# First phase of a conv, attention and FFN kernel: mask and scores in 64x64 array tiles, state matmuls behind them

## What is computed

```
t = circulant_inverse @ x                      # channel mixing, tokens x 128
h = layernorm(t)
Q, K = elu(h Wq) + 1, elu(h Wk) + 1            # 8 heads of 16
V = h Wv
out = causal linear attention:
      num_t = Q_t . sum_{s<=t} K_s V_s,  den_t = Q_t . sum_{s<=t} K_s
t = t + (num / den) Wo
t = t + FFN(layernorm(t))                      # weights merged per batch by a gate, 128 -> 512 -> 128, layernorm
```

## Time and profile before

| | us |
|---|---|
| median of 3 runs | 775.72 |
| lowest and highest | 775.37, 778.26 |
| span of the profiled execution | 776.8 |
| PE busy | 724.4 (93%) |
| DVE busy | 675.7 (87%) |
| ACT busy | 655.0 (84%) |
| POOL busy | 537.7 (69%) |

### The profile page before, as it was taken

One profiled execution on the slowest core, in us unless ns is written; L12 is line 12 of the kernel. 1 busy time (PEld: TensorE's weight loads), 2 busy tenths in 40 slices (PEclk: granted clock), 3 DMA queues, 4 the chain that ended last, 5 costly groups with the idle time before them and its releaser, 6 DMA issues. The chain is left out here.

```text
span 776.8 us, 38919 instructions
## 1 busy us (share of the span) xinstructions
PE 724.4 (93%) x11938; PEld 541.6 (70%) x11938; DVE 675.7 (87%) x2614; ACT 655.0 (84%) x1860; POOL 537.7 (69%) x1167
## 2 busy tenths in 40 slices
PE   4899989999999999999999999868999999999994
PEld 2566667777677777677777776657777788777773
DVE  5798979999999999999999999856889978898983
ACT  4688989999999999999999999745788886888883
POOL 3798979999999999999999999620333330333332
PEclk9999999999999999999999999988999999999997
DMA  4657765565665565565566564410122220222221
GB/s 142 112 117 120 125 119 132 135 138 126 135 142 128 131 141 131 128 138 134 126 138 134 125 146 105 97 33 27 40 76 79 80 81 16 83 81 81 81 81 68
DMA packets 202341, 82.57 MB, mean 106 GB/s; under 512 B 176076, under 2 KB 189551, under 8 KB 202232
## 3 DMA queue, kind: packets, MB, share of 16 engines
q1 hardware_dynamic: 202296, 81.99, 45.8%
HBM read 22.69 MB, written 17.30 MB: 51 GB/s over the span
## 5 line engine op out<-in xcount | busy, mean ns | idle before, releaser
L864 DVE SCALAR_TENSOR_TENSOR scores_lo<-p_a,scores_hi 128x512 f16<-128x512 f32 x256 | 176.1, 688 | 4.6 <-ACT scores_hi L750 1.1
L750 ACT ACTIVATE scores_hi<-p_a 128x512 f16<-128x512 f32 x256 | 156.4, 613 | 19.1 <-PE p_a L591 12.8
L1403 POOL TENSOR_TENSOR ffn_rstd_shift<-ffn_rstd_shift,consts 128x4 f32<-128x4 f32 x32 | 36.8, 1150 | 111.4 <-DVE ffn_rstd_shift L1361 111.4
L968 POOL CAST qk_parts<-qk_f 128x256 f16<-128x256 f32 x256 | 108.9, 427 | 6.0 <-issue 4.0
L978 POOL TENSOR_TENSOR qk_parts<-qk_f,qk_parts 128x128 f16<-128x128 f32 x256 | 104.0, 427 | 0.9
L1185 PE MATMUL psb<-merged_W_of_batch,h_hi 128*128 128x128 f16 x512 | 95.3, 222 | 2.2 <-DVE h_lo L1339 1.5
L1339 DVE TENSOR_TENSOR h_lo<-h_f,h_hi 128x512 f16<-128x512 f32 x128 | 95.9, 789 | 0.6 <-ACT h_hi L1241 0.6
L1187 PE MATMUL psb<-merged_W_of_batch,h_lo 128*128 128x128 f16 x512 | 94.9, 221 | 0.0
L1186 PE MATMUL psb<-merged_W_of_batch,h_hi 128*128 128x128 f16 x512 | 94.9, 221 | 0.0
L1230 ACT ACTIVATE h_f<-psb,merged_b_of_batch 128x512 f32<-128x512 f32 x128 | 87.1, 712 | 7.7 <-PE psb L1166 6.0
L608 PE MATMUL p_o<-v_parts,scores_hi 128*128 128x17 f16 x1024 | 90.1, 171 | 2.0 <-issue 0.2
(11 more groups left out here) (214 smaller groups left out, 2846.9 us busy)
## 6 DMA issues: line engine op xcount, KB each, us to landing
x_f<-in_x SPq DMA_DIRECT2D x32, 256.0 KB, 3.1
t_rows<-t SPq DMA_DIRECT2D x64, 128.0 KB, 2.1
t_back<-t_rows SPq DMA_DIRECT2D x32, 256.0 KB, 2.6
out<-out_tile SPq DMA_DIRECT2D x32, 256.0 KB, 2.0
tv_share<-in_L_ffn_tv_W SPq DMA_DIRECT2D x32, 128.0 KB
qkT_parts<-qk_parts SPq DMA_TRANSPOSE x128, 3.1
zT_hi_lo<-z_parts SPq DMA_TRANSPOSE x128, 2.3
merged_W<-in_L_ffn_W SPq DMA_DIRECT2D x2, 256.0 KB, 4.3
```

The costliest lines, as they stand in the source:

```text
L750: nc.scalar.activation(ah[:, t % 2, cols], p_a[:, cols], ACT.Relu).then_inc(ahi_ready[eo], 1)
L864: nc.vector.scalar_tensor_tensor(al[:, t % 2, cols], p_a[:, cols], 0.0, ah[:, t % 2, cols], ALU.max, ALU.subtract).then_inc(alo_ready[eo], 1)
L968: nc.gpsimd.tensor_copy(dst, src.unsqueeze(2).broadcast_to([P, NH, 2, DH])).then_inc(done, 1)
```

## The change

In the scores stage mask and scores are made in 64x64 tiles of the array. Keys are split in halves c = 0 (keys 0 to 63 of the tile) and c = 1 (keys 64 to 127). The mask is written only to the two diagonal blocks, four matmuls of 64x256 in place of two of 128x512. The scores are sixteen matmuls in place of eight: keys 0 to 63 against all 128 queries, keys 64 to 127 against queries 64 to 127. The block of late keys against early queries is never written; DVE clears partitions 64 to 127 of p_a once at the start of the phase (semaphore scores_cleared), and its zeros stay. In TENSOR_ORDER the scores stage now stands ahead of state. The waits for all four parts of the tile before (hi and lo of both halves) stand ahead of the first mask matmul. ACT, DVE and GpSimd lists, and the size of what they read, are the same.

```diff
@@ -39,7 +39,7 @@
 
 
 
-TENSOR_ORDER = [("state", 3), ("scores", 4), ("turn_out", 6), ("conv", 0), ("values", 5), ("out_project", 6),
+TENSOR_ORDER = [("scores", 4), ("state", 3), ("turn_out", 6), ("conv", 0), ("values", 5), ("out_project", 6),
                 ("project", 0), ("gate", 13)]
 SCALAR_ORDER = [("normalise", 10), ("relu_qk", 2), ("split_x", 0), ("tv_hi", 0), ("read_t1", 7), ("gate_relu", 14),
                 ("state_hi", 3), ("exp_qk", 1), ("scores_hi_0", 4), ("copy_out", 6), ("scores_hi_1", 4), ("v_hi", 1)]
...
@@ -578,21 +578,31 @@
 
                     def scores(b, t):
                         n = TILES * b + t
+                        read = n if isinstance(n, int) else pe.to_reg(n)
+                        turned = 32 * b + 16 * (t // 4 + 1)
+                        turned = turned if isinstance(turned, int) else pe.to_reg(turned)
+                        pe.wait_ge(scores_cleared, 1)
                         for eo in range(2):
-                            at_least(pe, ahi_ready[eo], n)
-                            at_least(pe, alo_ready[eo], n)
-                            mm(p_a[:, eo * 512:(eo + 1) * 512], identb[:, :],
-                               maskb[:, :].unsqueeze(1).broadcast_to([P, NP, P]),
-                               start=True, stop=False, skip_group_check=True)
-                        pe.wait_ge(qk_turned[t % 4], 32 * b + 16 * (t // 4 + 1))
+                            at_least(pe, ahi_ready[eo], read)
+                            at_least(pe, alo_ready[eo], read)
+                        for c in range(2):
+                            for eo in range(2):
+                                r, k = slice(64 * eo, 64 * eo + 64), slice(64 * c, 64 * c + 64)
+                                o = p_a[k, eo * 512:(eo + 1) * 512].rearrange("p (a q) -> p a q", a=NP)[:, :, k]
+                                mm(o, identb[r, r], maskb[r, r].unsqueeze(1).broadcast_to([64, NP, 64]),
+                                   start=True, stop=False, skip_group_check=True)
+                        pe.wait_ge(scores_cleared, 1)
+                        pe.wait_ge(qk_turned[t % 4], turned)
                         for a in range(NP):
-                            for eo in range(2):
-                                r, c0 = 64 * eo, eo * 512 + a * P
-                                last = mm(p_a[:, c0:c0 + P],
-                                          qkT[r:r + 64, t % 4, 1, a, :], qkT[r:r + 64, t % 4, 0, a, :],
-                                          start=False, stop=True, skip_group_check=True)
-                                if a == NP - 1:
-                                    last.then_inc(sc_done[eo], 1)
+                            for c in range(2):
+                                for eo in range(2):
+                                    r, k = slice(64 * eo, 64 * eo + 64), slice(64 * c, 64 * c + 64)
+                                    c0 = eo * 512 + a * P
+                                    last = mm(p_a[k, c0 + 64 * c:c0 + P],
+                                              qkT[r, t % 4, 1, a, k], qkT[r, t % 4, 0, a, 64 * c:P],
+                                              start=False, stop=True, skip_group_check=True)
+                                    if a == NP - 1 and c:
+                                        last.then_inc(sc_done[eo], 1)
 
                     def values(b, t):
                         n = TILES * b + t
@@ -896,6 +906,7 @@
                         dve.wait_ge(bn2, upto)
                         nc.vector.bn_aggr(st2[:, t % 4, 6:8], st2[:, t % 4, 0:6]).then_inc(mv2, 1)
 
+                    nc.vector.memset(p_a[64:P, :], 0.0).then_inc(scores_cleared, 1)
                     nc.vector.memset(p_s[:, :], 0.0).then_inc(state_cleared, 1)
                     def merged_w1(slot):
                         if slot == 0:
```

More of the change, by code:

```diff
@@ L390, in build @@
             (conv_done, in_done, bn1, mv1, ve1, rstd1, vhi_ready, exp_ready, relu_ready, vlo_ready,
-             qk_ready, qhi_ready, khi_ready, lo_ready, su_done, state_cleared, sh_ready, sp_ready,
+             qk_ready, qhi_ready, khi_ready, lo_ready, su_done, state_cleared, scores_cleared, sh_ready, sp_ready,
              av_done, den1, den2, o_ready, ot_done, oT_ready, wo_done,
@@ L395, in build @@
                     "conv_done in_done bn1 mv1 ve1 rstd1 vhi_ready exp_ready relu_ready vlo_ready "
-                    "qk_ready qhi_ready khi_ready lo_ready su_done state_cleared sh_ready sp_ready "
+                    "qk_ready qhi_ready khi_ready lo_ready su_done state_cleared scores_cleared sh_ready sp_ready "
                     "av_done den1 den2 o_ready ot_done oT_ready wo_done "
```

## The result

The changed kernel takes 825.77 us (median of 4 runs, 824.03 to 830.74), the kernel before 776.99 in the same comparison; the ratio is 1.0635, 95% interval 1.0601 to 1.0670. Slower, by 49 us; 824 was forecast. The profiled execution has a span of 828.9 us; it is the slowest of the four, 5 us above their median.

A forecast was written before the change was run, and what follows sets the result against it. Bound: p_a's round trip, lengthened by state matmuls, state_hi and exp_qk. Steady 90 x 4.04 + 13 x 4.33 = 419.9 against 379.4, +40.5; +5 earlier slots, +3 ends: +48.5 on 776.8, 825.3; median 1.1 lower, 824 us; range 784 to 852.

The forecast's parts named there:

- the round trip of p_a: Single-buffered score tile passing PE, ACT, DVE, back to the next mask: 3.18 us before, 4.04 with the new order.
- The walk: First-phase loop timed from mask start T through scores, state, state_hi, exp_qk and scores parts back to PE: 4.04 us.
- the clock: Rival: TensorE idling lowers its granted clock, adding up to 0.3 us a loop, up to 851 us; 0.11 shared with serial tiles.
- the term for steps of the sequencer and handing over: On TensorE, score matmuls handed over by T + 0.40, then four steps of 0.38 us: state matmuls at T + 0.78.
- The slots ahead: The 20 uneven slots before the steady ones: 20 x (4.04 - 3.80) = +5 us.
- the last few: The last few slots with scores, counted together with the first two: +3 us.
- One sign of being wrong: On TensorE: the forecast is wrong if state matmuls start within 0.5 us of the mask.
- The rival of prepared steps (786 us): TensorE's sequencer prepares steps behind the blocked mask: state matmuls at T + 0.87 end, loop 3.71 us, 786 us; chance 0.15.
- Tiles in turn (870 us): TensorE's 64x64 tiles run one after another: loop 4.49 us, about 870 us; chance 0.11 shared with slow clock.
- The gain that gets through (764 us): state_hi does not hold back scores_hi_0 on ACT; TensorE's saving shows until GpSimd's 3.57 us binds: 764 us; chance 0.08.
- The late transpose: Scores wait for qkT, landing 3.1 us after issue, needed 0.7 us earlier; binds only if slots stay short; no separate chance.

The follow-up runs named there:

- the new order with the state parts last: Changed kernel with state_hi served behind scores_hi_1 on ACT and state_lo behind scores_lo_1 on DVE: 775.29 us, ratio 0.9966.
- the doubling: state_hi made twice, the second waiting for the first: in the changed kernel (inside) 871.83 us; with state_hi and state_lo served behind the scores parts (outside) 797.97 us.
- the two edits that shortened a link: Changed kernel with DVE's mean_var1, denominator and eps1 moved behind scores_lo_1: 843.29 us; changed kernel with ACT's exp_qk moved behind scores_hi_1: 807.00 us.
- the version with adjacent parts: Changed kernel with DVE's mean_var1, denominator and eps1 moved behind scores_lo_1, so scores_lo_0 and scores_lo_1 adjoin: 843.29 us, ratio 1.0834.

## Why the prediction was right

**What binds.** The named mechanism was the round trip of p_a with the state matmuls, state_hi and exp_qk taken in. The old order with tiles (767.6), the new order with the state parts last (775.3) and the doubling (+46 us inside, +23 outside) show it: the cost goes and comes with that one dependence, not with the tiles, and, but for at most 8 us, not with TensorE's order as such. What the prediction did not have is the second branch, over state_lo and stats1 on DVE, which is only 0.18 us shorter than the way over exp_qk.

**The walk.** Forecast 4.04 us from mask to mask in slots with state matmuls. Measured are 3.93 to 4.10 in the 83 steady ones that kept the clock, 3.99 on the mean; and 4.33 for the slot without state matmuls, as forecast. The sum is nearer than its terms, and that is in part luck. In the slot shown above the state matmuls start at T + 0.51 (0.54 on the mean) where T + 0.78 was forecast: the term for steps of the sequencer and handing over was too large by about a quarter of a microsecond. (The sequencer is the part of the engine that hands over its instructions; a step is a semaphore wait or a register computation that it works off itself, PEldq in the profile.) I let the sixteen score matmuls be handed over no faster than the state's run and counted four steps. In the changed kernel the steps around the mask at 330.81 and the scores at 330.94 stand here, each with its count, durations in ns, first and last start:

```profile
L408 PEldq EVENT_SEMAPHORE  x1: 51/51/51, 330.7 to 330.7; - x1
L563 PEldq EVENT_SEMAPHORE  x1: 51/51/51, 331.0 to 331.0; - x1
L564 PEldq EVENT_SEMAPHORE  x1: 51/51/51, 331.1 to 331.1; - x1
L408 PEldq ALU_OP  x1: 32/32/32, 331.2 to 331.2; - x1
```

L563 is the state stage's first step. The hand-over of the scores takes about a tenth of a microsecond, and three steps of 0.1 follow, not four. Against that, two short terms were too small: from the end of scores_lo_1 to the mask 0.15 instead of 0.05 (the wait sits in a step of its own ahead of the weight load, the first row above), and on DVE 0.70 + 0.89 instead of 0.65 + 0.87. Net 3.94 for 4.04 in this slot.

For the steady part that makes 90 x 3.99 + 13 x 4.33 = 415 us where 419.9 was forecast, and the 6 us lost to the clock, which the forecast had kept as a rival and out of the sum, bring it to about the 422.1 measured. The slots ahead gave +7.9 and the last few +1.5 where +5 and +3 were put. So the profiled span is 3.6 us above the forecast one, while the medians of the timed runs agree within 2 us: this profile is of the slowest of the four runs. One sign of being wrong was nearly met: state matmuls within 0.5 us of the mask. They start 0.51 us behind it in the slot shown, and in a few slots 0.49. Whether the steps run ahead, which the sign was to tell, is read from the rows above: they do not.

**The rival of prepared steps (786 us)** is ruled out where it matters: the steps behind the blocked mask are not done in advance, L563 starts 0.2 us after the mask. But the reason differs from the one of the earlier trace rows, where a weight load was blocked: here the wait for scores_lo_1 is itself a step of the sequencer, and what stands behind it has to wait for it. The Trainium skill (Perfetto Trace Analysis, Sequencer Loop) has an engine instruction pushed into a queue, where it waits; the changed kernel does not test that, since the mask's wait is not in the queue. And of the 0.62 us that I charged from the first score matmul to the state matmuls, 0.24 was not there.

**Tiles in turn (870 us)** did not happen. Four masks of 256 columns take 0.13 us up to the scores; in turn they would take 0.44 by the prediction's estimate. The sixteen score matmuls start within 0.20 us (0.41 less the 0.21 of the last one), where eight took 0.18 before; the estimate in turn was 0.69. That the state matmuls come 0.38 us after the first score matmul is due to the steps in between. TensorE's own work ahead of turn_out is 331.68 - 330.81 = 0.87 us, forecast 0.81, before 1.22. By the Trainium skill (TensorEngine Tiling (Array Packing), Restrictions and Gotchas) column tiles go without Fast Weight Load. The slot does not show it: the sixteen score loads last 102 to 110 ns each, but all of them start between 330.91 and 331.08 us.

```profile
L601 PEld LDWEIGHTS p_a<-qkT_parts x16: 102/106/110, 330.9 to 331.1; 64*64 64x64 f16 x16
```

**The gain that gets through (764 us)** is what the old order with tiles gives, at 767.6: the price was right, and its condition, state_hi not holding back scores_hi_0, is what that run restores.

**The late transpose** shows no wait in the changed kernel between 200 and 400 us; with short slots it begins to (1.9 us of waits in the same 200 us in the version with the old order).

## What to carry to other kernels

With all engines 95% busy, look for the buffer with one copy and walk it once round, engine by engine; here its length against the slot told what the edit does, and the busy shares did not. When work is moved behind a stage that waits on such a buffer, everything that later queues wait for from that work joins the round trip, although no dependence was added. Walk every branch: shortening one gains only until the next one, as the two edits that shortened a link showed, on DVE (no gain) and on ACT (half of the 0.36 us). If a reorder loses, see which consumer order made it lose: here TensorE's list or those of ACT and DVE could be put right, and the tiles alone are a gain of 1.3%.

## What was not expected of the hardware

In the slot without state matmuls TensorE stood idle for 0.4 us before the mask and 0.75 us before turn_out, and around it the granted clock fell to about half (0.51, the level of 1.2 GHz) for some 3.4 us: three to seven times in 420 us from one execution of the changed kernel to the next, and not once in the steady part of the kernel before. In the doubled state_hi and in the version with adjacent parts it fell 18 and 22 times. The 64x64 matmuls run four at a time: from the first mask matmul to the first score matmul, four of 256 columns take 0.13 us, where two of 512 columns took 0.54. That includes a hole of 0.10 us, which the prediction reads as the change of array shape; the trace has a step of the sequencer in the same place (L601 in the kernel before, 51 ns, from 315.97 us; the scores start at 316.01), so what the change of shape itself costs is not shown.
